# A GRU's gate sums spread in 512-byte pieces, half a feed-forward tile moved to VectorE, and a longer warming of TensorE

## The reference, cut to what matters

```python
def _sparsify_2to4(h):                 # keep the 2 largest magnitudes of each 4
    g = h.reshape(B, S, I // 4, 4)
    _, idx = jax.lax.top_k(jnp.abs(g), 2)
    pos = jnp.arange(4)
    mask = (pos == idx[..., 0:1]) | (pos == idx[..., 1:2])
    return (g * mask.astype(g.dtype)).reshape(B, S, I)
h = silu(x @ w_gate) * (x @ w_up)      # 256 -> 1024
x = x + _sparsify_2to4(h) @ w_down     # 1024 -> 256

def cell(h, x):                        # GRU, 256 steps, each needs the state before
    gi = x @ W_ih + b_ih
    gh = h @ W_hh + b_hh
    i_r, i_z, i_n = jnp.split(gi, 3, axis=-1)
    h_r, h_z, h_n = jnp.split(gh, 3, axis=-1)
    r = sigmoid(i_r + h_r)
    z = sigmoid(i_z + h_z)
    n = tanh(i_n + r * h_n)
    h_new = (1.0 - z) * n + z * h
    return (h_new, h_new)
```

## Time and profile before

| | us |
|---|---|
| median of 3 runs | 1007.39 |
| lowest and highest of them | 1002.78, 1009.81 |
| the profiled execution, its own time | 1011.21 |
| its span, first to last instruction | 1008.9 |
| of it: before step 0 of the GRU | 329.5 |
| the GRU's 256 steps | 494 |
| what follows | 185 |

### The profile page before, as it was taken

One profiled execution on the slowest core, in us unless ns is written; L12 is line 12 of the kernel. 1 busy time (PEld: TensorE's weight loads), 2 busy tenths in 40 slices (PEclk: granted clock), 3 DMA queues, 4 the chain that ended last, 5 costly groups with the idle time before them and its releaser, 6 DMA issues.

```text
span 1008.9 us, 39463 instructions
## 1 busy us (share of the span) xinstructions
PE 774.1 (77%) x16555; PEld 512.8 (51%) x16648; DVE 612.4 (61%) x2104; ACT 476.6 (47%) x1905; POOL 414.0 (41%) x493
## 2 busy tenths in 40 slices
PE   3789977868997786967769597695666568999876
PEld 3444544445654564644546455464544445666554
DVE  5655555786647675676766667675675653343457
ACT  2523433376541564756656565564554533444231
POOL 0386670274136394592937739286002002211000
PEclk9999999899999897999999989998997999999989
DMA  8100000400000000000000000000013000000001
GB/s 252 32 1 2 2 1 1 156 1 1 2 22 11 4 5 12 5 15 4 8 11 4 13 4 13 6 5 14 4 17 115 4 3 1 2 1 2 1 1 42
DMA packets 33344, 20.14 MB, mean 20 GB/s; under 512 B 23953, under 2 KB 30097, under 8 KB 33169
## 3 DMA queue, kind: packets, MB, share of 16 engines
q1 hardware_dynamic: 27984, 17.04, 6.0%
q10 hardware_dynamic: 5184, 0.59, 0.4%
HBM read 14.47 MB, written 1.05 MB: 15 GB/s over the span
## 4 chain that ended last, share of the span: by engine, by line
PE 53%; DVE 24%; ACT 8%; issue 6%; SPq 2%; DMA 1%; POOL 1%; ACTq 0%; DVEq 0%; POOLq 0%
PE banks L1344 16%; PE banks L1289 5%; DVE work L1644 4%; DVE h_ring L1658 3%; PE banks L1314 3%; DVE gate_r L1640 3%; ACT nzh L1477 3%; DVE pre_n L1649 3%; PE banks L410 2%; PE banks L1688 2%; SPq L1269 2%; PE banks L385 2%; PE banks L318 2%; PE banks L1770 2%; PE banks L1744 1%
## 5 line engine op out<-in xcount | busy, mean ns | idle before, releaser
L1344 PE MATMUL banks<-w_qkv,h_ring 128*4 128x64 f32 x12288 | 233.2, 226 | 138.9 <-DVE h_ring L1658 125.4
L1344 PEld LDWEIGHTS banks<-w_qkv,h_ring 128*4 128x4 f32 x12288 | 182.9, 90 | 215.0 <-DVE h_ring L1658 197.3
L1468 ACT ACTIVATE banks<-gate_r 128x8 f32<-128x8 f32 x256 | 46.2, 181 | 186.7 <-DVE gate_r L1640 185.9
L1640 DVE STREAM_TRANSPOSE gate_r<-banks 128x64 f32<-128x64 f32 x256 | 64.0, 250 | 83.3 <-PE banks L1344 79.5
L1644 DVE STREAM_TRANSPOSE work<-banks 128x64 f32<-128x64 f32 x256 | 76.6, 299 | 6.8 <-PE banks L1344 6.5
L1658 DVE TENSOR_TENSOR_SCAN h_ring<-banks,nzh 128x24 f32<-128x24 f32 x256 | 52.9, 207 | 33.2 <-ACT nzh L1477 1.8
L1509 POOL TENSOR_TENSOR work<-work 128x512 f32<-128x512 f32 x14 | 17.8, 1271 | 127.4 <-ACT work L1405 127.4
L318 PE MATMUL banks<-zero 128*128 128x512 bf16 x192 | 61.9, 417 | 4.6 <-DVE work L2216 2.6
L1649 DVE TENSOR_TENSOR_SCAN pre_n<-banks,work 128x16 f32<-128x16 f32 x256 | 48.8, 191 | 27.3 <-DVE work L1644 1.4
L1473 ACT ACTIVATE gate_z<-banks 128x64 f32<-128x64 f32 x256 | 57.1, 223 | 12.6 <-PE banks L1344 12.2
L1651 DVE STREAM_TRANSPOSE banks<-gate_z 128x64 f32<-128x64 f32 x256 | 60.7, 237 | 2.9 <-ACT gate_z L1473 0.8
(11 more groups left out here) (446 smaller groups left out, 1651.5 us busy)
## 6 DMA issues: line engine op xcount, KB each, us to landing
big<-in_x SPq DMA_DIRECT2D x1, 1024.0 KB, 5.8
w_gate<-in_L_ffn_w_gate SPq DMA_DIRECT2D x1, 1024.0 KB, 4.9
shared<-in_L_ffn_w_down SPq DMA_DIRECT2D x1, 1024.0 KB, 7.5
w_gate<-in_L_ffn_W SPq DMA_DIRECT2D x1, 1024.0 KB, 5.5
shared<-in_L_ffn_W SPq DMA_DIRECT2D x1, 1024.0 KB, 10.4
out_x<-big SPq DMA_DIRECT2D x4, 256.0 KB, 2.4
w_qkv<-in_L_cond_W_qkv SPq DMA_DIRECT2D x1, 768.0 KB, 7.2
w_qkv<-in_L_attn_W_qkv SPq DMA_DIRECT2D x1, 768.0 KB, 9.0
```

Source lines behind the costliest of these rows:

```text
L1344: mm = nc.tensor.matmul(bank[32 * j:32 * j + B, 0:64], h_col(t, c), w_hh[:, c, g, :].rearrange("p (m n) -> p m n", m=KC)[:, :, 32 * j:32 * ...
L1640: nc.vector.transpose(gate_r[:, :], bank_r[:, 0:64]).then_inc(g_tr, 1)
```

## The change

What it does:

- `g_tok` is laid out by column block: `rows_out` writes its 128 sums as four runs of 32, at [block j][gate and half n][32], so that the 128 values of block j lie together. `spread` then moves one piece of 512 B per token instead of four of 128 B. Number of DMAs, bytes and destination layout of `g_row` in bytes are as before.
- Tile 1, half 0: ScalarE's `gate_copy` and `up_copy` and GpSimd's `multiplied` go; VectorE reads PSUM itself (`multiplied_at_once(v, chain, 1, 0)`) and makes the absolute value and the three comparisons (`compared`) right after tile 0's pruning, ahead of `grown(0, ...)`. The counting and masking (`counted`, `kept_of`) stay where the whole pruning stood. Semaphore counts are adjusted (`e_gc`, `e_uc` by two, `e_hid`, `e_free`).
- `keep_warm(24, bank_b)` becomes `keep_warm(40, bank_b)`.

The diff, cut to its core:

```diff
         def spread(op, tile, b, j):
-            return op.dma_start(g_row[tile % 2][32 * j + b:32 * j + b + 1, :, :, :].rearrange("p u g (m n) -> p u (g m) n", m=KC),
-                                g_tok[tile % 2][32 * b:32 * b + 32, :].rearrange("u (g n) -> u g n", g=4)[:, :, 32 * j:32 * j + 32]).then_inc(g_g2, 16)
+            return op.dma_start(g_row[tile % 2][32 * j + b:32 * j + b + 1, :, :, :].rearrange("p u g n -> p u (g n)"),
+                                g_tok[tile % 2][32 * b:32 * b + 32, P * j:P * (j + 1)]).then_inc(g_g2, 16)
...
-            keep_warm(24, bank_b)
+            keep_warm(40, bank_b)
...
-                if tile == 0:
+                if tile == 0 or (tile, n) == (1, 0):
                     a.then_inc(e_gc, 1)
...
-                nc.scalar.copy(kept[:, 512 * n:512 * (n + 1)], (bank_b, bank_a)[n][:, :]).then_inc(e_uc, 1)
+                nc.scalar.copy(kept[:, 512 * n:512 * (n + 1)], (bank_b, bank_a)[n][:, :]).then_inc(e_uc, 2 if tile == 1 else 1)
...
             gate_sigmoid(1, 0)
-            gate_copy(1, 0)
             by_hidden_out(0, 0)
-            up_copy(1, 0)
             by_hidden_out(0, 1)
...
+        def pruned(v, chain, tile, n):
+            compared(v, chain, tile, n)
+            counted(chain, n)
+            kept_of(n)
...
-            for n in range(2):
-                multiplied(pool, nc.gpsimd, chain, 1, n)
+            multiplied(pool, nc.gpsimd, chain, 1, 1)
             pruned_pool(pool, chain, 1, 1)
...
-                return nc.vector.tensor_tensor(g_tok[tile % 2][:, P * n:P * (n + 1)], bank_a[:, P * n:P * (n + 1)],
-                                               bias_rz[:, P * n:P * (n + 1)], ALU.add).then_inc(g_gd, 1)
+                cols = lambda a: a[:, P * n:P * (n + 1)].rearrange("p (j x) -> p j x", j=4)
+                return nc.vector.tensor_tensor(g_tok[tile % 2].rearrange("p (j g x) -> p j g x", j=4, g=4)[:, :, n, :], cols(bank_a),
+                                               cols(bias_rz), ALU.add).then_inc(g_gd, 1)
...
             for n in range(2):
-                multiplied_at_once(v, chain, n)
+                multiplied_at_once(v, chain, 0, n)
                 pruned(v, chain, 0, n)
+            multiplied_at_once(v, chain, 1, 0)
+            compared(v, chain, 1, 0)
             for m in range(KC):
                 grown(0, m)
             for n in range(4):
                 rows_out(0, n)
...
-            pruned(v, chain, 1, 0)
+            counted(chain, 0)
+            kept_of(0)
```

More of the change, by code:

```diff
@@ L1497, in build, with multiplied_at_once @@
         quad = lambda a: a.rearrange("p (g e) -> p g e", e=4)
-        def multiplied_at_once(v, chain, n):
+        def multiplied_at_once(v, chain, tile, n):
             h, s = (a[:, 512 * n:512 * (n + 1)] for a in (hid, sgm))
-            v.wait_ge(e_gc, n + 1)
+            v.wait_ge(e_gc, 2 * tile + n + 1)
             chain.done(nc.vector.tensor_tensor(h, (bank_d, bank_c)[n][:, :], s, ALU.mult))
-            v.wait_ge(e_up, n + 1)
+            v.wait_ge(e_up, 2 * tile + n + 1)
             nc.vector.tensor_tensor(h, (bank_b, bank_a)[n][:, :], h, ALU.mult).then_inc(e_free, 1)
@@ L1511, in multiplied, with compared @@
             op.tensor_tensor(h, h, k, ALU.mult).then_inc(e_hid, 1)
-        def pruned(eng, chain, tile, n):
-            op = nc.vector
[L1515 to L1520, removed]
+        def pruned(v, chain, tile, n):
+            compared(v, chain, tile, n)
+            counted(chain, n)
+            kept_of(n)
+        def compared(v, chain, tile, n):
+            op = nc.vector
+            h, ab = (a[:, 512 * n:512 * (n + 1)] for a in (hid, sgm))
+            one, two, three = (a[:, P * n:P * (n + 1), :] for a in (c1p, c2p, c3p))
+            v.wait_ge(e_free, 2 * tile + n + 1)
             chain.done(op.tensor_scalar(ab.bitcast(I32), h.bitcast(I32), 0x7FFFFFFF, None, ALU.bitwise_and))
-            a4, h4 = quad(ab), quad(h)
+            a4 = quad(ab)
             op.tensor_tensor(one[:, :, 1:4], a4[:, :, 0:3], a4[:, :, 1:4], ALU.is_ge)
@@ L1525, in pruned, with counted @@
             chain.done(op.tensor_tensor(three, a4[:, :, 0:1], a4[:, :, 3:4], ALU.is_ge))
+        def counted(chain, n):
+            op = nc.vector
+            one, two, three, w = (a[:, P * n:P * (n + 1), :] for a in (c1p, c2p, c3p, win))
             chain.done(op.tensor_tensor(w, one[:, :, 1:5], one[:, :, 0:4], ALU.subtract))
@@ L1530, in pruned, with kept_of @@
             chain.done(op.tensor_tensor(w[:, :, 3:4], w[:, :, 3:4], three, ALU.subtract))
+        def kept_of(n):
+            h4, k4 = (quad(a[:, 512 * n:512 * (n + 1)]) for a in (hid, kept))
+            w = win[:, P * n:P * (n + 1), :]
             for e in range(4):
-                a = op.scalar_tensor_tensor(quad(k)[:, :, e:e + 1], w[:, :, e:e + 1], float(2 - e), h4[:, :, e:e + 1], ALU.is_ge, ALU.mult)
+                a = nc.vector.scalar_tensor_tensor(k4[:, :, e:e + 1], w[:, :, e:e + 1], float(2 - e), h4[:, :, e:e + 1], ALU.is_ge, ALU.mult)
             a.then_inc(e_kept[n], 1)
@@ L1540, in pruned_pool @@
             one, two, three, w = (a[:, P * n:P * (n + 1), :] for a in (c1p, c2p, c3p, win))
-            pool.wait_ge(e_hid, 2 * tile + n - 1)
+            pool.wait_ge(e_hid, 2 * tile + n - 2)
             chain.done(op.tensor_scalar(ab, h, 0.0, 2.0, ALU.is_ge, ALU.mult))
```

## The result

The changed kernel takes 991.36 us (median of 4 runs, 987.16 to 996.90) against 1005.09 us before (4 runs, 1001.89 to 1009.81), measured together: ratio 0.9853, 95% interval [0.9807, 0.9899]. It is faster by 1.5%. Predicted were 1000.0 us, with 992 to 1006; the direction was right, the size too small.

A forecast was written before the change was run, and what follows sets the result against it. The prediction saw a recurrence without slack, 1.853 us a quiet step; only slower steps and the stretch before step 0 could move. From the profiled 1011.2 us, -5.6 - 0.7 - 4.7 = -11.0 gave 1000.2; predicted 1000.0, range 992 to 1006.

The forecast's parts named there:

- GpSimd's multiplications: Before step 0: taking tile 1, half 0 from GpSimd frees VectorE's pruning and removes TensorE's wait, -1.4 us.
- The clock dip of 1.0 us: Before step 0: without TensorE's 1.40 us wait the clock would not fall in the down projection, -1.0 us.
- The issue at 0.48 us: Spreads: with longer pieces each issue on ACT would take 0.48 us instead of 0.67.
- The landing at 3.9 us: Spreads before step 0: landing 3.9 us after the last issue began, instead of 4.68.
- The warming sets step 0: Before step 0: 40 fillers end at 325.8, after the spreads; start -3.7 us, held clock -1.9, together -5.6.
- half of the stretches: Recurrence: of 9.4 us in three low-clock stretches tied to the spreads' traffic, half goes, -4.7 us.
- rival A: Recurrence: all three low-clock stretches beside spreads go, -9.4 us, giving 995.5 us; chance 0.22.
- Rival B: Spreads: short pieces cost nothing between SBUF and SBUF, so issue, landing and loop stay; 1003.1 us; chance 0.17.
- C: Recurrence: the clock falls at all seven tile boundaries, three more costing +9.4 us, giving 1011.2 us; chance 0.08.
- D: Before step 0: GpSimd locks VectorE in its new block and the first dip stays; 1002.9 us; chance 0.08.
- The discount for the median: Whole kernel: median 3.8 us under the profiled execution, about one low-clock stretch, so less to take there.
- T: Theory of the experiments: TensorE's waits for its own instructions and the clock falls behind them come from the spreads' traffic.

The follow-up runs named there:

- e7: The changed kernel without the moved pruning: GpSimd multiplies both halves of tile 1, VectorE prunes half 0 after rows_out, as before; 994.91 us, ratio 0.9870.
- e5: The kernel before with only the new layout (spread and rows_out), 24 fillers and pruning as they were; 993.18 us, ratio 0.9842.
- e1: The changed kernel with the old 128 B pieces (g_tok, rows_out and spread as before); 1008.02 us, ratio to before 0.9958.
- e10: The changed kernel with 40 fillers and the last 3 MB of loads paced as twelve small loads; 986.33 us, ratio 0.9792.
- e11: The changed kernel with paced loads and 24 fillers instead of 40; 987.50 us, ratio 0.9786.
- e3: The changed kernel with 24 fillers instead of 40 before step 0; 989.88 us, ratio 0.9857.
- e2: The changed kernel with the old 128 B pieces in odd tiles only, 512 B in even ones; 998.44 us, ratio 0.9907.
- e6: The changed kernel with pieces of 256 B, 80 packets a spread; 990.64 us, ratio 0.9822.
- e9: The changed kernel with eight added 64 KB copies a tile (tiles 1 to 7) in 512 B pieces, which nothing reads; 1022.87 us, ratio 1.0146.
- e4: The changed kernel with the last 3 MB of weight loads held back until step 231; 986.80 us, ratio 0.9817.
- e8: The changed kernel with the last 3 MB of weight loads cut into twelve, one for every second step; 987.46 us, ratio 0.9799.

## Why the prediction was too small, point by point

**GpSimd's multiplications: right.** VectorE's pruning was no longer held up beside GpSimd (0.43 us at L1521), and TensorE's wait of 1.40 us went. e7 prices the move at 1.6 us.

**The clock dip of 1.0 us: not shown, and the reason given was wrong.** The changed kernel has no dip there, but e7 has the wait and no dip either, and the kernel before and e5 have both (2.98 and 3.07 us). What brings it in some profiles stays open.

**VectorE's new block: right.** It ended at 312.7, 0.3 us later than worked out, and `grown` ran at once. GpSimd's multiplication began 0.2 us before the end of its last comparison and did not hold it up. Later GpSimd does: in `counted`, L1531 takes 1.41 us beside GpSimd's L1551 against 0.29 in the first pruning, but that lies under the spreads' flight, as predicted.

**rows_out at nothing: right.** Four instructions took 0.88 us, 0.89 before.

**The issue at 0.48 us: wrong.** It is 0.65 us on ACT (4.58 us for 7) and 0.63 on SP (5.04 for 8), about as at 128 pieces (0.67 and 0.65 in e1). The load of 128 rows was the wrong neighbour. **The landing at 3.9 us: wrong the other way.** It is 2.3 us. The two errors nearly cancel: seeds were due at 324.5 and came at 323.9. **The 0.7 us wait for spreads in the loop: right in size, wrong in reason.** It went, but SP's twelve issues took 8.09 us instead of 5.8, which leaves the earlier landing as the reason.

**The warming sets step 0: right in time, wrong in worth.** Predicted first matmul 325.8, measured 325.61; the first steps are 1.84 us apart. The start gained 4.9 us to the first scan, with the slow steps behind it about 6.3 by the profiles; 5.6 was the term. But the gain is not the warming's alone, for the quicker transfer covers it: with the seeds there at 323.9, 24 fillers do as well within what 6 runs tell (e10, e11), for TensorE then idles 2 us instead of 4.7. Counted alike, with the slow steps, the moved pruning with 40 fillers and old pieces (e1) gains 5.4 us at the start, with 24 fillers and new pieces (e3) 6.7.

**The step that failed: half of the stretches.** I saw that all seven waits of TensorE on its instructions stood beside spreads or loads, priced the three stretches beside spreads at 9.4 us, and took half, as a third of the packets carries the same bytes. e1 and e2 show that with short pieces they are there and without them they are not: all of it goes. Small stalls in the spread windows that I had left out (three of 0.7 to 0.9 us) went too. In the profiles the loop gained 15.4 us instead of 5.4. That is rival A, at which I had put 0.22, with more than its price. A was also reckoned from the profiled 1011.2 us, while B, C and D start from the median 1007.4; from the median it would have been 991.7.

**The discount for the median: wrong.** I took the 3.8 us between the profiled execution and the median for one stretch less, so for less to take. But e1, which has the new start and the old pieces, has a ratio of 0.9958 against 0.9853, which is 10.6 us (16.7 us between the medians of all runs): the usual run pays for most or all of these waits. Much of the scatter is elsewhere: the phases before GpSimd's memset take 290.3 to 296.4 us in the profiles of e6 and e11, on identical instructions.

**Rival B** (no gain from longer pieces between SBUF and SBUF) falls by e1 and e5. The rule of the Trainium skill ("DMA: Bandwidth & Descriptors", Why small descriptors are slow) by which it argued does not hold for the landing of these transfers: pieces of 128 B land 2.3 us later than pieces of 512 B, and the measurement decides. The pace at which packets start did not suffer: in tile 0, e1's 2304 began within 5.1 us, the changed kernel's 768 within 5.0. From the last packet's start to the seeds it was 2.9 us in e1, and 0.8 in the changed kernel and with 256 B. **C** falls: one low-clock stretch, not seven. **D**: the lock that it feared did not occur in the new block.

**What carries T, and what stays open.** The DMA queues of e1 in the microsecond from 682 (packets, MB, their time as a share of 16 engines' microsecond); q8 brings one packet of instructions, 16 KB:

```profile
q8 instruction: 1, 0.02, 17.3%
q1 hardware_dynamic: 148, 0.02, 10.8%
q10 hardware_dynamic: 144, 0.02, 10.6%
```

The same queue in the kernel before, in the microsecond from 386; this packet began 0.7 us after the last one of a tile's spreads:

```profile
q8 instruction: 1, 0.02, 18.2%
```

And in e1 in the quiet, in the microsecond from 692:

```profile
q8 instruction: 1, 0.02, 9.0%
```

17.3% of 16 us is 2.8 us, 18.2% is 2.9, for a packet that takes 1.4 us in the row from the quiet, where the mean is 0.9 and the longest 1.5. Over six spread windows of 14 us, a packet of instructions takes 1.58 us on average in e1, 1.12 in the changed kernel, 1.14 with 256 B and 1.07 in e9. So packets of instructions take longer beside short pieces.

The spreads' own landings are late in the same places. From the start of a tile's last packet to its last landing, tiles 1 to 6, the traces' semaphore records (some are missing, which can make a value too small) give 0.7 to 1.0 us in the changed kernel, 0.7 to 1.7 with 256 B, 0.9 to 3.4 in e1 and 1.7 to 4.6 in the kernel before; in e2 2.5, 6.2 and 4.5 in odd tiles, and 0.7, 0.9 and 1.1 in even ones. TensorE's longest waits overlap with the long ones: in e1, 686.0 to 690.4 with 688.4 to 691.8, in e2, 499.0 to 501.9 with 501.0 to 507.1.

That late instructions are TensorE's wait is argued from place and time and not shown. The rows name no queue of TensorE's, and the packet shown of e1 had ended at 685.7, before TensorE stood still. Beside the 3 MB of loads the argument has less: the packets of instructions there took 1.1 us at most in the changed kernel, and TensorE waited 2.6 us all the same. Why a 128 B piece does this and a 256 B piece hardly does is open, and so is why a wait of over 1 us drops the clock at one place (1.3 us, e5's last, with slow steps behind it) and not at another (1.1 us in e4).

## What to carry to other kernels

Look at what a transfer does to the engines that don't wait for it: a DMA that lands in time may still hold up an engine that does not wait for it. Where an engine waits on "issue" only beside certain transfers, lengthen their pieces and spread out bulk loads before touching the compute; test it by changing the pieces in every second tile of one kernel. And when a stall's place points to its causes seven times out of seven, as here to spreads or loads, price the edit at the whole of it, with nothing as the other end, not at half.

## What the runs showed of the hardware that was not expected

- The issue of a 16 KB copy from 32 partitions into one took 0.63 to 0.67 us ahead of step 0 with 32, 64 or 128 pieces alike; the landing after the last issue fell from 4.7 to 2.3 us between 128 and 256 B (seeds' idle 8.5 us in e1, 6.3 with 256 B, 6.2 with 512 B), and no further. The packets started as fast; what took longer lay behind the last one's start (2.9 us against 0.8).
- Three loads of 3 MB in all made TensorE wait 2.6 us and lose its clock for three more steps; the same bytes in twelve loads cost 0.2 us (e8).
- 40, 30 or 24 filler matmuls ahead of a wait of 7 us made no difference that 6 runs can tell.
